# A recommendation kernel on one core: a semaphore for each group of gathered rows, row numbers ahead of two memsets, and the last layers interleaved with the last tile's weighted sum

## The reference

```python
seq_embed = concat([emb_seq[i][seq_inputs[:, :, i]] for i in range(2)])        # 2048 x 40 x 128
item_embed = concat([emb_seq[i][item_inputs[:, i]] for i in range(2)])
q = broadcast_to(item_embed[:, None, :], seq_embed.shape)
info = concat([q, seq_embed, q - seq_embed, q * seq_embed])
h = sigmoid(sigmoid(info @ att_W1 + att_b1) @ att_W2 + att_b2)
att = softmax(where(mask, (h @ att_Wf + att_bf)[..., 0], NEG_INF))
user_info = einsum('bl,bld->bd', att, seq_embed)
info_all = concat([user_info, item_embed, dense, sparse_0, sparse_1, sparse_2])
info_all = bn_gamma * (info_all - bn_mean) * rsqrt(bn_var + 1e-3) + bn_beta
info_all = prelu(info_all @ ffn_W1 + ffn_b1, ffn_a1)
info_all = prelu(info_all @ ffn_W2 + ffn_b2, ffn_a2)
return sigmoid(info_all @ out_W + out_b)
```

## Time and profile before

| | |
|---|---|
| Median of 3 runs | 1632.27 us |
| The profiled execution | 1632.64 us, its span 1630.6 us |
| PE busy | 1421.3 us (87%) |
| PEld busy | 784.2 us (48%) |
| DVE busy | 857.2 us (53%) |
| ACT busy | 399.8 us (25%) |
| POOL busy | 1208.6 us (74%) |
| Chain that ended last, by engine | POOL 56%, issue 24%, DMA 14%, PE 4%, DVE 1%, ACT 1% |
| Mean granted TensorE clock | 0.971 |

### The profile page before, as it was taken

The page is one execution under the profiler, slowest core; times in us unless marked ns, Lnnn a source line. Parts: engine busy times, 40 slices in busy tenths (PEclk is TensorE's granted clock), DMA queues, the critical chain, the costliest instruction groups (busy, mean ns, idle before and its releaser), DMA issues.

```text
span 1630.6 us, 22953 instructions
## 1 busy us (share of the span) xinstructions
PE 1421.3 (87%) x7680; PEld 784.2 (48%) x7680; DVE 857.2 (53%) x2118; ACT 399.8 (25%) x726; POOL 1208.6 (74%) x1269
## 2 busy tenths in 40 slices
PE   0599999989999998888989989898988989898868
PEld 0355555545545445554545545454544545454432
DVE  5744647463544646464464635446463644646443
ACT  3422213122212112221221222121122212212223
POOL 6877777777777777777777777777777777777772
PEclk9999999999999999999999999999999999999975
DMA  7411121211112121111212111121212112121121
GB/s 161 103 27 47 27 47 27 46 28 33 41 27 47 27 46 29 39 35 27 47 28 46 27 43 31 27 47 27 46 29 44 30 27 47 28 46 27 27 27 9
DMA packets 59523, 64.11 MB, mean 39 GB/s; under 512 B 33477, under 2 KB 33811, under 8 KB 59407
## 3 DMA queue, kind: packets, MB, share of 16 engines
q0 software_dynamic: 40448, 41.50, 14.7%
q1 hardware_dynamic: 16898, 12.98, 2.8%
q10 hardware_dynamic: 2062, 8.08, 1.9%
HBM read 62.36 MB, written 0.11 MB: 38 GB/s over the span
## 4 chain that ended last, share of the span: by engine, by line
POOL 56%; issue 24%; DMA 14%; PE 4%; DVE 1%; ACT 1%; POOLq 0%; DVEq 0%; ACTq 0%
POOL hist L332 54%; DMA hist<-in_L_rec_emb_seq_dram,idx 14%; POOL items L332 2%; PE grown L405 1%; DVE sums L875 1%; PE pre L525 1%; PE pre L526 1%; ACT pool L622 0%; PE sums L537 0%; PE turned L518 0%; DVE hist L725 0%; PE turned L519 0%; PE pre L440 0%; PE pre L442 0%; PE mid L449 0%
## 5 line engine op out<-in xcount | busy, mean ns | idle before, releaser
L332 POOL DMA_INDIRECT hist<-in_L_rec_emb_seq_dram,idx x1184 | 1132.0, 956 | 360.9 <-issue 333.7
L405 PE MATMUL grown<-pool,split 128*128 128x384 bf16 x4782 | 863.3, 330 | 39.7 <-DVE pool L778 39.6
L405 PEld LDWEIGHTS grown<-pool,split 128*128 128x128 bf16 x4782 | 461.6, 99 | 452.1 <-issue 158.1
L778 DVE TENSOR_SCALAR pool<-rel 128x768 bf16<-128x768 bf16 x800 | 389.8, 540 | 0.0
L902 DVE TENSOR_TENSOR prod_t<-turned,item_t 128x512 f32<-128x512 f32 x160 | 109.5, 688 | 399.5 <-ACT hist_t L647 398.7
L652 ACT ACTIVATE hidden<-pre 80x512 f32<-80x512 f32 x160 | 94.9, 593 | 619.5 <-DVE pre L910 619.5
L910 DVE TENSOR_TENSOR pre<-pre,item_part 80x512 f32<-80x512 f32 x160 | 110.8, 692 | 171.8 <-PE pre L442 171.8
L423 PE MATMUL turned<-ident,hist 128*128 128x128 f32 x592 | 100.4, 291 | 86.2 <-POOLq L360 75.6
L440 PE MATMUL pre<-hist_t,w_hist 128*80 128x512 f32 x320 | 163.7, 593 | 0.0
L442 PE MATMUL pre<-prod_t,w_raw 128*80 128x512 f32 x320 | 163.4, 592 | 0.0
L875 DVE SCALAR_TENSOR_TENSOR sums<-hist,weight,sums 128x128 f32<-128x128 f32 x608 | 159.7, 346 | 0.0
(11 more groups left out here) (110 smaller groups left out, 469.6 us busy)
## 6 DMA issues: line engine op xcount, KB each, us to landing
hist<-in_L_rec_emb_seq_dram,idx POOLq DMA_INDIRECT x1184, 2.4
keys<-key_rows SPq DMA_DIRECT2D x30, 384.0 KB, 4.4
hist<-in_L_rec_emb_seq_dram ACTq DMA_DIRECT2D x6, 672.0 KB
keys<-key_rows ACTq DMA_DIRECT2D x4, 384.0 KB, 7.2
hist<-in_L_rec_emb_seq_dram ACTq DMA_DIRECT2D x2, 728.0 KB
sparse_rows<-in_L_rec_emb_sparse_dram,idx_sparse POOLq DMA_INDIRECT x48, 3.4
raw<-in_r_seq_inputs_dram SPq DMA_DIRECT2D x1, 600.0 KB, 4.6
hist<-in_L_rec_emb_seq_dram ACTq DMA_DIRECT2D x6, 90.0 KB
```

The costliest lines, as they stand in the source:

```text
L332: gp.indirect_dma_start(rows, None, table, bass.IndirectOffsetOnAxis(ap=index, axis=0)).then_inc(landed, 16)
L405: last = nc.tensor.matmul(grown[n][:, 0:MC], split[n][:, c, k, :], hot[:, slot, n * MC:(n + 1) * MC], start=(c == 0 and k == 0), stop=(c = ...
L778: last = nc.vector.tensor_scalar(hot[:, slot, :], rel[half][:, :, 0:RC], float(c), None, ALU.is_equal)
```

## The change

It has three parts.

1. Each of the 10 groups has a semaphore of its own for each of the two halves of the buffer. The gathers count it up, and PE waits for it. POOL's wait and its `nop` in the midst of a group go, and with them `group_ready`.
2. On DVE only the first of the three clears stays ahead of the row numbers; the other two follow them. `table_cleared` counts each clear, and ACT loads piece q after clear q.
3. The last layers of pair 0 start on PE as soon as the last tile's scores have been read (`softmax_step` at its last count). DVE does `prelu1(0)` between the two steps of the last tile's weighted sum, and `prelu2(0)` behind the user vector. `turn_user` and `part_of` move to PE's iterations for pairs 2 and 3 (`USER_AT`), since only pair 7 needs the last tile's `part`. The output matmul writes to `pre1[1]`, since `sums` is still in use, and the sparse rows are turned into `turned[1]`. The loops of ACT and DVE over the pairs are written out.

```diff
+    USER_AT = 2
-        group_landed = [sem(f"group_landed{s}") for s in range(2)]
-        eighth_landed = [sem(f"eighth_landed{h}") for h in range(2)]
-        last_landed = [sem(f"last_landed{h}") for h in range(2)]
+        group_landed = [[sem(f"group{g}_landed{h}") for g in range(GROUPS)] for h in range(2)]
...
                         for k in range(NB if g == LAST else G * NB):
-                            if 0 < g < LAST and k == 6:
-                                used = (LAST - 1) // 2
-                                gp.wait_ge(group_landed[(g - 1) % 2], 16 * G * NB * (tile * used + (g - 1) // 2 + 1))
-                                gp.nop(nofuse=True).then_inc(group_ready, 1)
                             c = g * G * NB + k
-                            gather(hist[:, half, c * E:(c + 1) * E], seq_table, idx[half][:, c:c + 1], landed)
+                            gather(hist[:, half, c * E:(c + 1) * E], seq_table, idx[half][:, c:c + 1],
+                                   group_landed[half][g])
...
-                    if g < LAST - 1:
-                        pe.wait_ge(group_ready, tile * (LAST - 1) + (g + 1))
-                    elif g == LAST - 1:
-                        pe.wait_ge(eighth_landed[half], 16 * G * NB * (pair + 1))
-                    else:
-                        pe.wait_ge(last_landed[half], 16 * NB * (pair + 1))
+                    pe.wait_ge(group_landed[half][g], 16 * NB * (1 if g == LAST else G) * (pair + 1))
...
-            turn_user(TILES - 1)
-            part_of(TILES - 1, 1)
-            pe.wait_ge(part_ready, TILES)
...
-                nc.tensor.matmul(sums[0:1, 0:W], ow[:, :], y2[:, :], start=True, stop=True).then_inc(score_done, 1)
+                nc.tensor.matmul(pre1[1][0:1, 0:W], ow[:, :], y2[:, :], start=True, stop=True).then_inc(score_done, 1)
+            pe.wait_ge(softmax_step, TILES * 2)
             for p in range(PAIRS):
                 turn_sparse(p)
...
                     output(p - 1)
+                if p == USER_AT:
+                    turn_user(TILES - 1)
+                if p == USER_AT + 1:
+                    part_of(TILES - 1, 1)
...
-            act.wait_ge(table_cleared, 1)
             for q in range(SLOTS):
+                act.wait_ge(table_cleared, q + 1)
                 load_piece(q)
...
-            final_user(TILES - 1, 1)
-            final_part(TILES - 1)
...
-            copy_sparse(0)
-            with act.Fori(1, PAIRS) as p:
+            for p in range(PAIRS):
                 copy_sparse(p)
-                add_bias2(p - 1)
-                score_of(p - 1)
+                if p > 0:
+                    add_bias2(p - 1)
+                    score_of(p - 1)
+                if p == USER_AT:
+                    final_user(TILES - 1, 1)
+                if p == USER_AT + 1:
+                    final_part(TILES - 1)
...
+            def clear(k):
+                nc.vector.memset(staged[k][3 * P // 4:P, :, :], 0.0).then_inc(table_cleared, 1)
-            for k in range(SLOTS):
-                last = nc.vector.memset(staged[k][3 * P // 4:P, :, :], 0.0)
-            last.then_inc(table_cleared, 1)
+            clear(0)
...
             row_numbers(0, 0)
+            for k in range(1, SLOTS):
+                clear(k)
...
-            for step in range(len(ROWS_AT)):
-                add_rows(TILES - 1, 1, step)
...
                 dve.wait_ge(ffn1_done, p + 1)
+                dve.wait_ge(part_ready, 2 * p + 2)
...
-            dve.wait_ge(part_ready, TILES)
-            prelu1(0)
-            with dve.Fori(1, PAIRS) as p:
+            for step in range(len(ROWS_AT)):
+                add_rows(TILES - 1, 1, step)
+                if step > 0:
+                    prelu2(step - 1)
+                prelu1(step)
+            for p in range(len(ROWS_AT), PAIRS):
                 prelu2(p - 1)
                 prelu1(p)
             prelu2(PAIRS - 1)
```

More of the change, by code:

```diff
@@ L201, in build @@
         sparse_landed = [sem(f"sparse_landed{p}") for p in range(PAIRS)]
-        group_landed = [sem(f"group_landed{s}") for s in range(2)]
-        eighth_landed = [sem(f"eighth_landed{h}") for h in range(2)]
-        last_landed = [sem(f"last_landed{h}") for h in range(2)]
+        group_landed = [[sem(f"group{g}_landed{h}") for g in range(GROUPS)] for h in range(2)]
         lane_numbered = sem("lane_numbered")
         fold_ready = sem("fold_ready")
-        group_ready = sem("group_ready")
         group_turned = sem("group_turned")
@@ L347, in _ @@
                     for g in range(GROUPS):
-                        if g == LAST:
-                            landed = last_landed[half]
-                        elif g == LAST - 1:
-                            landed = eighth_landed[half]
-                        else:
-                            landed = group_landed[g % 2]
                         if g == PACE:
@@ L517, in turn_sparse @@
                     rows = sparse_rows[:, 2 * p + h, :]
-                    nc.tensor.transpose(turned[0][:, h * P:(h + 1) * P], rows[:, 0:2 * E], ident[:, :])
-                    last = nc.tensor.transpose(turned[0][0:SPARSE_B[1], W + h * P:W + (h + 1) * P], rows[:, 2 * E:NS * E],
+                    nc.tensor.transpose(turned[1][:, h * P:(h + 1) * P], rows[:, 0:2 * E], ident[:, :])
+                    last = nc.tensor.transpose(turned[1][0:SPARSE_B[1], W + h * P:W + (h + 1) * P], rows[:, 2 * E:NS * E],
                                                ident[:, :])
@@ L700, in copy_sparse @@
                 k = SPARSE_B[1]
-                normalised(x_sparse[:, 0, :], 3, turned[0][:, 0:W])
-                normalised(x_sparse[0:k, 1, :], 4, turned[0][0:k, W:2 * W]).then_inc(sparse_copied, 1)
+                normalised(x_sparse[:, 0, :], 3, turned[1][:, 0:W])
+                normalised(x_sparse[0:k, 1, :], 4, turned[1][0:k, W:2 * W]).then_inc(sparse_copied, 1)
             def add_bias2(p):
@@ L708, in score_of @@
             def score_of(p):
-                wait(act, score_done, p + 1)
-                nc.scalar.activation(score[:, bass.ds(p * W, W)], sums[0:1, 0:W], ACT.Sigmoid, bias=ob[:, :])\
+                act.wait_ge(score_done, p + 1)
+                nc.scalar.activation(score[:, p * W:(p + 1) * W], pre1[1][0:1, 0:W], ACT.Sigmoid, bias=ob[:, :])\
                     .then_inc(score_ready, 1)
-            copy_sparse(0)
-            with act.Fori(1, PAIRS) as p:
+            for p in range(PAIRS):
                 copy_sparse(p)
-                add_bias2(p - 1)
-                score_of(p - 1)
+                if p > 0:
[5 more added lines that the diff above has]
+                    final_part(TILES - 1)
             add_bias2(PAIRS - 1)
@@ L964, in _ @@
                     body(pair * 2 + half, half, pair, False)
-            for step in range(len(ROWS_AT)):
-                add_rows(TILES - 1, 1, step)
             def prelu1(p):
                 dve.wait_ge(ffn1_done, p + 1)
-                nc.vector.tensor_tensor(z1[:, :], pre1[0][0:H1, 0:W], part[:, bass.ds(p * W, W)], ALU.add).then_inc(z1_step, 1)
+                dve.wait_ge(part_ready, 2 * p + 2)
+                nc.vector.tensor_tensor(z1[:, :], pre1[0][0:H1, 0:W], part[:, p * W:(p + 1) * W], ALU.add).then_inc(z1_step, 1)
                 dve.wait_ge(z1_step, 2 * p + 1)
```

## The result

The changed kernel takes 1620.92 us (median of 4 runs, 1620.25 to 1621.74) against 1632.78 of the kernel before, run beside it: a ratio of 0.9924 with a 95% interval of 0.9908 to 0.9940, 11.9 us less. The forecast was 1621.0. The profiled execution took 1620.25 us with a span of 1618.2, against 1632.64 and 1630.6: 12.4 us less in the profiles.

A forecast was written before the change was run, and what follows sets the result against it. POOL's start, pitch and stalls were taken to bound the kernel up to 1541 us, the last layers after that. 1632.64 - 0 - 3.4 - 8.0 = 1621.2, 1620.9 against the median; forecast 1621.0, range 1617.5 to 1625.5.

The forecast's parts named there:

- Part 1: Group semaphores between gathers and PE, in place of POOL's waits and nops: claimed to change the time by 0 us.
- My 0.01 us: Release of PE's turns: cost of going by POOL, from turns 2.55 and 2.54 us after their last gathers.
- The rival in which POOL needs its own brake: POOL's gathers: without waits the pitch grows, for example to 1.27 us, ending at 1648 us; chance 0.03.
- Part 2: Start of the kernel: row numbers before two clears let POOL's gathers begin 3.4 us earlier, between 0.6 and 5.4.
- the value 0 for the clears: First two gathers: clears running beside them were taken to delay them by 0 us, against a possible 0.8.
- The 2 us that I left for this: Early gathers beside DVE's table work: stalls kept at 15 us, with 2 us allowed either way.
- Part 3: End of the kernel: last layers beside the weighted sum, claimed -8.0 us, from 10.35 less 2.35.
- the term of the two inserted pieces: PE's pair loop at the end: `part_of` adds about 1.95 us and `turn_user` 0.4, together 2.35.
- The rival of the upper clock: Last pairs: PE at 2.4 GHz, cycles about 3.4 us instead of 5.30, end about 1610 us; chance 0.04.
- my sign of 0.50 throughout: Last layers on PE: the granted clock was expected to stay at 0.50 throughout, its lower level of 1.2 GHz.
- The rival of late handovers: Last layers: `ffn1(0)`, with 0.7 us of room, comes late and they gain little, 1626 to 1629.5 us; chance 0.04.
- What would be late next: Pair 7 at the end: its sparse rows land at 1604.2, before a turn at 1610.8, leaving 6.6 us of room.

The follow-up runs named there:

- e1: The kernel before with only the group semaphores added: 1633.78 us, ratio 0.9999 to the kernel before.
- e2: The kernel before with only the row numbers moved first: 1629.98 us, ratio 0.9978 to the kernel before.
- e3: The kernel before with only the last layers put beside the weighted sum: 1625.7 us, ratio 0.9946 to the kernel before.
- e7: The changed kernel with idle bf16 matmuls in PE's waits ahead of pair 2 and 6 in each later pair: 1613.75 us over 4 runs.
- e5: The changed kernel with the weighted sum cut finer, so pairs 0 to 2 do not wait for all of it: 1615.36 us.
- e8: The changed kernel with the finer weighted sum of e5 and 14 idle matmuls in pair 0, 6 in each later pair: 1615.12 us.

## Why the prediction was right

- **What bounds the kernel.** Right: POOL's start, pitch and stalls carry through 1530 us unchanged (3.47 us at the first gather, 3.48 at group 8's last), and the other gain is after the last gather.
- **Part 1, nothing.** Right, and tested alone: a ratio of 0.9999. PE's side could be read in the trace of before, where both kinds of release stood side by side. My 0.01 us came from one pair of turns, and turns released by the DMA alone start 2.44 to 2.56 us after their last gather, so the detour's cost is known to about 0.1 us only. The rival in which POOL needs its own brake is out: the pitch stayed at 1.249 us in `e1`. One reading in my text was wrong without weight: there are 48 sparse gathers and not 38 (44 of them took 0.94 or 0.95 us, four 1.08 or 1.09).
- **Part 2, -3.4 us.** Right: -3.48 in the profile, -3.6 in `e2`. The input was there in time, and the value 0 for the clears holds, on the two gathers beside them. The stalls came out the same, 14.90 and 14.95 us over 50 gathers, in these two profiles. That is chance: `e1` has 16.1, `e2` 15.5 and `e3` 16.4, where the same DVE instructions fall a little differently against the gathers. The 2 us that I left for this were about right.
- **Part 3, -8.0 us.** The mechanism was right and the size short by 0.9: -8.90 in the profile, -8.8 in `e3` by the ratio. `turn_sparse(2)` came 10.66 us earlier for my 10.35: 0.1 us of this up to the end of the user vector, and 0.2 in `prelu2(0)`, which began 0.08 us before that end and took 0.80 us for my 0.9. The larger part is the term of the two inserted pieces, 2.35 in my sum: the cycles with `turn_user` and `part_of` are 0.26 and 1.74 us longer than 5.30 (5.56 and 7.04), and the last pair's way to the output is 0.19 shorter (9.78 for 9.97). The loops are written out there; which instruction saves the 0.19 is not shown.
- **How near the number came.** The forecast of 1621.0 and the median of 1620.92 are nearer than the working deserves. Against the profile the sum was 0.95 us off (1621.2 for 1620.25), nearly all of it in part 3, and the runs of the changed kernel lie up to 1.5 us apart.
- **The rival of the upper clock.** It did not come about from pair 1 on: 0.50 from 1567.6 to the end. Only the turn and `ffn1` of pair 0 still ran at 1.00, where the two L505 matmuls took 0.66 us for 1.14, so my sign of 0.50 throughout did not hold for them. What stood against the rival, a busy PE at 0.50 in the earlier trace rows, is confirmed, and the other side is shown: with idle bf16 matmuls the same pairs run at 1.00 and 4.07 us a cycle. My text gave 3.4 us for such a cycle without its working, and no run shows one without idle matmuls. An estimate from the profiled one of the four runs of `e7` agrees with it: `ffn1` began at 1599.93, after the idle matmuls, but ACT's copy that it needs had ended at 1599.19, so about 0.7 of its 4.1 us could go.
- **The rival of late handovers.** Out: `prelu1(0)` begins at 1569.29, as the first 18 additions end (1569.32). `ffn1(0)` ended at 1567.53, so the room was 1.8 us for my 0.7. Part of it came from the upper clock: in `e5` the same `ffn1(0)` took 2.21 us at the lower one for 1.25 here, and 0.8 would have been left.
- **What would be late next.** Right in kind: PE waited for the sparse rows of pair 7, 0.9 us in one of the runs of `e7` and 3.8 in `e8`. The room in the changed kernel was 5.4 us (last gather at 1597.84, landing 3.4 us later, turn at 1606.66) for my 6.6.

## What to carry to other kernels

Look for two instances of the disputed thing in the trace that you have: here one release by POOL and one by the DMA, as far behind their gathers within 0.1 us, gave the forecast for the change's first part, and `e1` bore it out. A chain of waits may name a transfer that costs nothing, when the wait stands behind queued work; ask whether the engine ever stood idle longer than between two other pieces of work. When two independent ends of a kernel are changed, their gains add only as far as the next limit, so compute that one too: here it stood 5.4 us away, and two further gains of 5.5 and 7 us together met it. An engine that reaches such a limit earlier waits longer, and in `e8` it came out of the wait at the lower clock.

## What was not expected of the hardware

- A PE that reads as busy 9.8 of 10 us can stay at a granted clock of 0.50 for 30 us: the pairs' f32 matmuls do so in both kernels (1590 to 1620 before, 1580 to 1610 after). Six bf16 matmuls of 128x384 in each cycle, beside its own twelve, went with a clock of 1.00 from 1590 on (`e7`). Extra work that nobody uses made the kernel 7 us faster.
- The stalls of gathers beside two-input DVE instructions depend on small shifts: between 14.6 and 16.5 us in the ten profiles that have all sixteen instructions. Two profiles of one kernel, those of `e7`, have 14.85 and 16.19 us, and their times are 1612.85 and 1614.12: the 1.3 us by which they differ is that of the stalls. Whether this is the cause of all the scatter between runs was not tested.
- A held gather ends about 0.82 us (0.81 to 0.85 in all traces) after the DVE instruction that held it last, wherever it was caught, and a gather that started before the instruction, or within 0.03 us of its start, is not held.
